# One product stage moved ahead of the mode sums, and an inverse transform split into five jobs, in a Fourier-layer kernel on one core

## The chip, the core and the metric

The kernel runs on 1 core of one Trainium2 chip. The metric is the device time of one launch in microseconds (us); less is better. TensorE does the matrix products (PE in the rows, PEld its weight loads), VectorE (DVE) and ScalarE (ACT) move and transform results, SyncE (SP) issues the transfers, and GpSimd (POOL) does almost nothing here. Everything is float32. One f32 product of the program is two matmul records and two weight-load records in the trace.

## What is computed

Thirty-two images of 8 x 256 x 256 go through two blocks, each added to its input. The first is a group norm and a masked 3x3 convolution with a hidden layer of 32. The second, which fills most of the time, is a group norm, a lift to 4 groups of 10 channels, four Fourier layers, and two pointwise products:

```
for i in range(4):
    h1 = _spectral_conv(h, sp_w1[i], sp_w2[i])
    h2 = _gconv1x1(h, w_w[i], w_b[i])
    h = h1 + h2
    if i < 3:
        h = _gswish(h, betas[i])
h = _gswish(_gconv1x1(h, fc1_w, fc1_b), betas[3])
return _gconv1x1(h, fc2_w, fc2_b)
```

`_spectral_conv` is a real 2D Fourier transform of which 24 x 12 modes are kept, a 10 x 10 complex product per group and mode, and the inverse transform. `_gconv1x1` is the mixing of the 10 channels of a group at each pixel.

## The kernel before

An image is worked through at a time, in a loop of 32 turns that all five engines run. Each engine has its own list of instructions, in an order written out by hand, and semaphores between them. For TensorE the order of one image is: the convolution (8 units), the first forward transform, then the four Fourier layers (`lay` 0 to 3), then fc1 and fc2 (128 steps).

A Fourier layer 1 to 3 begins with the spectrum that the layer before left. TensorE does `rows(lay, False)` and `rows(lay, True)` (L624), the second half of the forward transform, into bank 0. VectorE scales that (L1072 to L1074) and makes ten products of spectrum and weights (`next_modes`, L811), four buffers in a ring. TensorE adds them up as they come, in `mode_sums` (L555 and L558, 288 products of 24 per call of `summed`, 12 calls), into bank 1. Then VectorE copies the sums out and adds the bias (`mixed`, L1026, L1028), and for even layers turns them by a quarter (L1031 to L1038). While it does, TensorE runs `spin`, products whose result nobody reads (L566, bank 2).

The next stage is the one that the change is about, the inverse rows. `inverse_rows(lay)` makes 40 products (L588 in even layers, L584 in odd ones) in three jobs: job 0 into banks 0 to 3, job 1 into banks 4 to 7, job 2 (half as long) into banks 0 and 1. Each job is emptied into the tile `gst` by both engines at once, half of its banks each: ScalarE at L771, VectorE at L1046 (`inverse_kept`, whose slices come from `inverse_part`). Job 2 waits until job 0 has been emptied.

Then come 11 pixel units, `pixels(lay)`. A unit is a mixing part (L666, 16 products, the pointwise product of the layer on `hmem`, or on `lifted` in layer 0) and a Fourier part (L674, 8 products out of `gst`) that adds into the same four banks, 4 to 7 for even units and 0 to 3 for odd ones. ScalarE turns the four banks into the next `hmem` (L792). The mixing part of unit 0 waits for the emptying of job 1, whose banks it takes, and its Fourier part for the emptying of job 2. After unit 10 come `columns` (L605) and `rows`, which start the next layer.

`inverse_banks(t, engine)` says which banks an engine empties in job t, and `pixel_bank(lay, u)` which bank a unit begins with. The semaphore `s_g` counts jobs done, `s_gA` and `s_gD` jobs emptied by ScalarE and VectorE.

The functions in question, with the lines of the profile:

Of the kernel before, what the change touches and what calls it, by code (L numbers as in the profile page):

```python
# [14 lines left out]
LAYERS = 4  # L15
# [4 lines left out]
ROW2 = 2 * W  # L20
# [134 lines left out]
def program(nc, nb, x, conv1_w, conv1_b, conv2_w, conv2_b, lift_t, lift_b, lift_g, mix_w, mix_b, spec_w, betas,  # L155
            fc1_w, fc1_b, fc2_w, fc2_b, fwd_row, turn_id, fwd_col, inv_row, inv_col, grid, gridf, gmean, signs, out):
    with ExitStack() as ctx:
# [101 lines left out]
        WSP = 16 * 16  # L259

# [35 lines left out]
        def inverse_banks(t, engine):  # L296

            first, count = 4 * (t % 2), 4 if t < 2 else 2
            return (first, first + count // 2) if engine == 0 else (first + count // 2, first + count)

        def inverse_part(t, engine):

            b0, b1 = inverse_banks(t, engine)
            o = 4 * t + b0 % 4
            return (bass.AP(gst, NBLK * YY * o, [[128 * YY, 128], [NBLK * YY, b1 - b0], [32 * YY, 4], [1, NBLK * YY]]),
                    bass.AP(PS, 512 * b0, [[4096, 128], [512, b1 - b0], [NBLK * YY, 4], [1, NBLK * YY]]))
# [159 lines left out]
        def _(pe):  # L466
# [19 lines left out]
            with pe.Fori(0, nb) as i:  # L486
# [82 lines left out]
                def inverse_rows(lay):  # L569

                    n = (i * 4 + lay) * 3
                    pe.wait_ge(s_ot, i * 4 + lay + 1)
                    pe.sem_inc(s_bank, 1)
                    for t in range(3):
                        bank, count = 4 * (t % 2), 4 if t < 2 else 2
                        if t == 2:
                            pe.wait_ge(s_gA, n + 1)
                            pe.wait_ge(s_gD, n + 1)
                            pe.sem_inc(s_bank, 1)
                        for g in range(G):  # L580
                            for a in range(count):
                                p, ch = 64 * (a % 2), 5 * g + 2 * t + a // 2
                                if lay % 2:
                                    mm = nc.tensor.matmul(PS[32 * g:32 * g + MODES, bank + a, 0:4 * NBLK * YY],  # L584
                                                          rot[p:p + 32 + KX, ch, 0, 0:MODES], invr[p:p + 32 + KX, :], start=True,
                                                          stop=True, tile_position=(p, 32 * g))
                                else:
                                    mm = nc.tensor.matmul(PS[:, bank + a, NBLK * YY * g:NBLK * YY * g + NBLK * YY],  # L588
                                                          rot[p:p + 32 + KX, ch, :, :].rearrange("p c m -> p (c m)"),
                                                          invr[p:p + 32 + KX, 0:NBLK * YY], start=True, stop=True,  # L590
                                                          tile_position=(p, 0), skip_group_check=True)
                        mm.then_inc(s_g, 1)
# [48 lines left out]

                def pixels(lay):

                    for u in range(PU):
                        at = pixel_bank(lay, u)
                        if u >= 2:
                            before = u if at != pixel_bank(lay, u - 2) else u - 1
                            pe.wait_ge(s_hrow, i * (4 * PU) + (lay * PU + before))
                            if lay == LAYERS - 1:
                                pe.wait_ge(s_hlast, i * PU + before)  # L650
# [3 lines left out]
                        if lay == 0 and u in (0, 4):  # L654
                            pe.wait_ge(s_lnorm, i * 2 + 1 + u // 4)
                        pe.sem_inc(s_bank, 1)
                        for r in range(4):
                            for s in range(4):
                                if lay == 0:
                                    w, src = compw[32 * r:32 * r + 28, s, :], lifted[32 * r:32 * r + 28, u * ROW2:u * ROW2 + ROW2]  # L660
                                else:
                                    src = hmem[32 * r:32 * r + 30, s * PART + u * ROW2:s * PART + u * ROW2 + ROW2]
                                    w = mix13[32 * r:32 * r + 30, lay // 2, :]
                                if lay == 2:
                                    w = mix2[32 * r:32 * r + 30, s, :]
                                nc.tensor.matmul(PS[32 * s:32 * s + 32, at + r, :], w, src, start=True, stop=True,  # L666
                                                 tile_position=(32 * r, 32 * s))
                        if u == 0:
                            pe.wait_ge(s_gA, (i * 4 + lay) * 3 + 3)
                            pe.wait_ge(s_gD, (i * 4 + lay) * 3 + 3)  # L670
# [19 lines left out]
                for lay in range(LAYERS):  # L690
                    if lay:
                        mode_sums(lay)
# [47 lines left out]
        def _(act_):  # L740
# [26 lines left out]
            def inverse_kept(i, lay):  # L767
                for t in range(3):
                    act_.wait_ge(s_g, (i * 4 + lay) * 3 + (t + 1))
# [36 lines left out]
        def _(dve):  # L806
# [235 lines left out]
            def inverse_kept(i, lay):  # L1042
                for t in range(3):
                    dve.wait_ge(s_g, (i * 4 + lay) * 3 + (t + 1))
# [161 lines left out]
```

## Time and profile before

| | us |
|---|---|
| three runs | 17366.53, 17488.7, 17523.27 |
| their median | 17488.7 |
| the profiled execution | 17363.02 |
| its span, first to last instruction | 17361.2 |
| TensorE busy in it | 16419.9 (95%) |
| ScalarE busy | 11026.2 (64%) |
| VectorE busy | 6269.9 (36%) |
| mean granted TensorE clock | 0.971 |

The profiled execution is near the fastest of the three runs; the runs lie 157 us apart. Busy matmul time is modelled and says only that the engine had work in flight. A unit of work that comes once in each layer of each image comes 128 times, so 1 us there is 128 us, and 1 us in one layer of each image is 32 us.

### The profile page before, as it was taken

What the parts mean: (1) busy time and instruction counts of PE and PEld (TensorE: products, weight loads), DVE (VectorE), ACT (ScalarE), POOL (GpSimd) and SP (SyncE); (2) the same over time, 40 slices, a digit from 0 to 9 for tenths busy, and PEclk for the clock granted to TensorE, in tenths of its full rate; (3) what the DMA queues carried; (4) which work ended last, traced back from release to release, by engine and by line L of the source; (5) the groups of instructions that cost most, each with busy time, mean ns of one, the idle gap of its engine ahead of it and who ended that gap; (6) DMA issues with size and microseconds to landing.
All of it is one profiled execution on the core that took longest, in us unless ns stands there. A gap on an engine that the chain in (4) does not pass through costs nothing.

```text
span 17361.2 us, 558419 instructions
## 1 busy us (share of the span) xinstructions
PE 16419.9 (95%) x246998; PEld 6564.6 (38%) x246998; DVE 6269.9 (36%) x7495; ACT 11026.2 (64%) x10372; POOL 55.3 (0%) x69
## 2 busy tenths in 40 slices
PE   4999999999999999999999999999999999999999
PEld 2334433344433444333443334443344433344333
DVE  4234442234422344323443224442234432344322
ACT  1765567765576655676556676557665567655667
POOL 0000000000000000000000000000000000000000
PEclk9999999999999999999999999999999999999999
DMA  1111111111111111111111111111111111111111
GB/s 44 42 33 44 38 37 45 35 41 38 41 39 42 36 40 38 40 42 33 43 38 38 42 35 43 38 41 39 42 36 41 37 40 43 33 42 38 38 42 34
DMA packets 512312, 681.11 MB, mean 39 GB/s; under 512 B 90930, under 2 KB 483338, under 8 KB 493718
## 3 DMA queue, kind: packets, MB, share of 16 engines
q1 hardware_dynamic: 507318, 642.88, 14.4%
q8 instruction: 2046, 33.52, 0.8%
q14 instruction: 540, 4.42, 0.1%
q10 hardware_dynamic: 2408, 0.28, 0.0%
HBM read 507.57 MB, written 135.27 MB: 37 GB/s over the span
## 4 chain that ended last, share of the span: by engine, by line
PE 92%; DVE 4%; issue 2%; DVEq 1%; ACTq 1%; ACT 0%; SPq 0%; DMA 0%
PE PS L702 26%; PE PS L717 24%; PE PS L674 10%; PE PS L666 9%; PE PS L605 7%; PE PS L494 5%; PE PS L555 2%; PE PS L558 2%; PE PS L588 2%; PE PS L504 1%; PE PS L566 1%; PE PS L584 1%; PE PS L527 1%; PE PS L480 1%; PE PS L624 1%
## 5 line engine op out<-in xcount | busy, mean ns | idle before, releaser
L799 ACT ACTIVATE work<-PS 128x512 f32<-128x512 f32 (+1 forms) x8192 | 7939.5, 1021 | 762.9 <-PE PS L702 255.6
L702 PE MATMUL PS<-hmem,fcw 31*128 31x512 f32 x32768 | 4713.9, 645 | 106.9 <-DVE hmem L1109 45.4
L717 PE MATMUL PS<-work,fcw 128*32 128x512 f32 x32768 | 4398.8, 609 | 35.1 <-ACT work L799 33.4
L702 PEld LDWEIGHTS PS<-hmem,fcw 31*128 31x128 f32 x32768 | 1289.0, 184 | 3508.4 <-ACT work L799 3356.5
L792 ACT ACTIVATE hmem<-PS 128x2048 f32<-128x2048 f32 x1056 | 1983.1, 1878 | 663.6 <-PE PS L674 663.6
L1052 DVE STREAM_TRANSPOSE work<-hmem 128x2048 f32<-128x2048 f32 x864 | 1997.3, 2312 | 452.9 <-ACT hmem L792 405.8
L771 ACT ACTIVATE gst<-PS 128x528 f32<-128x528 f32 (+1 forms) x384 | 201.5, 539 | 2782.8 <-PE PS L584 1678.5
L674 PEld LDWEIGHTS PS<-invc,gst 24*128 24x128 f32 x22528 | 1495.7, 330 | 1189.1 <-issue 1188.5
L674 PE MATMUL PS<-invc,gst 24*128 24x256 f32 x22528 | 1917.8, 454 | 0.0
L717 PEld LDWEIGHTS PS<-work,fcw 128*32 128x32 f32 x32768 | 650.9, 108 | 3203.8 <-ACT work L799 3038.3
L1115 DVE SCALAR_TENSOR_TENSOR work<-PS,f2b,work 128x512 f32<-128x512 f32 x224 | 168.2, 751 | 4625.3 <-PE PS L717 4625.3
L666 PE MATMUL PS<-hmem,mix 30*32 30x512 f32 x33792 | 1228.7, 604 | 21.9 <-DVE gst L1046 21.9
L605 PE MATMUL PS<-work,fcol 32*24 32x512 f32 x30720 | 1183.4, 551 | 11.5 <-issue 10.3
L1115 DVE SCALAR_TENSOR_TENSOR wspec<-PS,f2b,wspec 128x512 f32<-128x512 f32 x128 | 96.1, 751 | 2935.7 <-PE PS L717 2935.7
L494 PE MATMUL PS<-work,c1w 32*64 32x512 f32 (+1 forms) x12288 | 824.7, 650 | 109.1 <-issue 95.3
L555 PE MATMUL PS<-work,sums 128*32 128x120 f32 x10240 | 720.7, 297 | 176.2 <-DVE work L811 164.6
L779 ACT ACTIVATE hmem<-PS,c1b 128x1024 f32<-128x1024 f32 x256 | 285.0, 1113 | 925.2 <-PE PS L494 925.2
L558 PE MATMUL PS<-work,sums 128*32 128x60 f32 x20480 | 723.5, 233 | 57.1 <-issue 56.7
L605 PEld LDWEIGHTS PS<-work,fcol 32*24 32x24 f32 x30720 | 641.8, 96 | 355.1 <-issue 134.1
L558 PEld LDWEIGHTS PS<-work,sums 128*32 128x32 f32 x20480 | 677.2, 118 | 88.0 <-issue 87.0
L555 PEld LDWEIGHTS PS<-work,sums 128*32 128x32 f32 x10240 | 617.7, 117 | 224.6 <-DVE work L811 189.8
L794 ACT ACTIVATE hmem<-PS 128x1024 f32<-128x1024 f32 x352 | 360.3, 1024 | 508.9 <-PE PS L674 508.9
(130 smaller groups left out, 9430.4 us busy)
## 6 DMA issues: line engine op xcount, KB each, us to landing
work<-in_x SPq DMA_DIRECT2D x1518, 128.0 KB, 2.5
wspec<-in_spec_w SPq DMA_DIRECT2D x768, 90.0 KB, 2.1
hmem<-x_d SPq DMA_DIRECT2D x128, 528.0 KB
x_d<-work SPq DMA_DIRECT2D x512, 128.0 KB, 2.9
wspec<-in_spec_w SPq DMA_DIRECT2D x768, 60.0 KB, 2.0
fcw<-fcw_d SPq DMA_DIRECT2D x32, 960.0 KB, 5.2
work<-x_d SPq DMA_DIRECT2D x384, 64.0 KB
wspec<-x_d SPq DMA_DIRECT2D x384, 64.0 KB
```

The lines of the kernel that those rows point to most:

```text
L494: mm = nc.tensor.matmul(to[:, :, lo:hi], c1w[32 * r:32 * r + 32, dx, :], rows[32 * r:32 * r + 32, 2 * u:2 * u + 2, lo + dx - 1:hi + dx - 1 ...
L555: nc.tensor.matmul(to[64 * t:64 * t + 32], sums[:, 0, pick, :], by[:, :, t:WID:2, :, s], start=begin, stop=end, tile_position=(0, 64 * t), ...
L558: mm = nc.tensor.matmul(to[64 * t + 32:64 * t + 64, 1 - r], sums[:, r, pick, :], by[:, r, t:WID:2, :, s], start=begin and r == 0, stop=end ...
L605: mm = nc.tensor.matmul(to, fcol[32 * r:32 * r + 32, b, :], part[32 * r:32 * r + 32, :, :, b, :], start=b == 0, stop=b == 7, tile_position ...
L666: nc.tensor.matmul(PS[32 * s:32 * s + 32, at + r, :], w, src, start=True, stop=True, tile_position=(32 * r, 32 * s))
L674: mm = nc.tensor.matmul(PS[:, at + r, y * W:y * W + W], gst[32 * r:32 * r + MODES, :, :, 2 * u + y].rearrange("p s o -> p (s o)"), invc[32 ...
L702: mm = nc.tensor.matmul(PS[:, fc_bank(p, r), :], f1w[32 * r:32 * r + 31, k, g, :], hmem[32 * r:32 * r + 31, g * PART + u * ROW2:g * PART + ...
L717: mm = nc.tensor.matmul(PS[32 * c:32 * c + 32, 7, :], f2w[:, k, g, :], act[p % 2][:, c * ROW2:c * ROW2 + ROW2], start=kg == 0, stop=final, ...
L792: nc.scalar.activation(unit(u), PS[:, at:at + 4, :], ACT.Silu).then_inc(s_hrow, 1)
L794: nc.scalar.activation(unit(u)[:, 0:2], PS[:, at:at + 2, :], ACT.Identity).then_inc(s_hrow, 1)
L799: nc.scalar.activation(act[p % 2][:, strips], PS[:, bank:bank + (3 if rest else 1), :].rearrange("p a b -> p (a b)"), ACT.Silu).then_inc(s ...
L1052: V.transpose(to, unit(u)).then_inc(s_tr, 1)
```

## The change

The inverse rows are done in five jobs of two banks instead of three jobs of four, four and two. Job t takes banks 0 and 1 if t is even and 2 and 3 if it is odd, and ScalarE empties the first of the two, VectorE the second. Jobs 2, 3 and 4 each wait until the job two before has been emptied. Banks 4 to 7 are free of the inverse rows. The mixing part of a unit is now a function of its own, `mix(lay, u)`. For layers 1 to 3 that of unit 0 is called ahead of `mode_sums(lay)`, into banks 4 to 7, where it lies until its Fourier part adds to it; in layer 0 it stays where it was, behind the inverse rows. The Fourier part of unit 0 waits until job 4 has been emptied, in all layers. The products are the same ones, in number and shape.

```diff
-            first, count = 4 * (t % 2), 4 if t < 2 else 2
-            return (first, first + count // 2) if engine == 0 else (first + count // 2, first + count)
...
+            return (bass.AP(gst, NBLK * YY * (2 * t + engine), [[128 * YY, 128], [32 * YY, 4], [1, NBLK * YY]]),
+                    bass.AP(PS, 512 * (2 * (t % 2) + engine), [[4096, 128], [NBLK * YY, 4], [1, NBLK * YY]]))
...
-                    pe.sem_inc(s_bank, 1)
-                    for t in range(3):
-                        bank, count = 4 * (t % 2), 4 if t < 2 else 2
-                        if t == 2:
-                            pe.wait_ge(s_gA, n + 1)
-                            pe.wait_ge(s_gD, n + 1)
-                            pe.sem_inc(s_bank, 1)
+                    for t in range(JOBS):
+                        if t >= 2:
+                            pe.wait_ge(s_gA, n + (t - 1))
+                            pe.wait_ge(s_gD, n + (t - 1))
+                        pe.sem_inc(s_bank, 1)
                         for g in range(G):
-                            for a in range(count):
-                                p, ch = 64 * (a % 2), 5 * g + 2 * t + a // 2
+                            for a in range(2):
+                                p, ch, bank = 64 * a, 5 * g + t, 2 * (t % 2) + a
...
                 def pixels(lay):

                     for u in range(PU):
                         at = pixel_bank(lay, u)
...
+                        if u or lay == 0:
+                            mix(lay, u)
                         if u == 0:
-                            pe.wait_ge(s_gA, (i * 4 + lay) * 3 + 2)
-                            pe.wait_ge(s_gD, (i * 4 + lay) * 3 + 2)
...
+                            pe.wait_ge(s_gA, (i * 4 + lay) * JOBS + JOBS)
+                            pe.wait_ge(s_gD, (i * 4 + lay) * JOBS + JOBS)
                             pe.sem_inc(s_bank, 1)
...
                     if lay:
+                        mix(lay, 0)
                         mode_sums(lay)
                     spin(2, 3 if lay % 2 == 0 else 1)
                     inverse_rows(lay)
```

## Rows read from the trace of the kernel before

**Rows 1.** The page's head, and its first lines of busy time and chain.

```profile
span 17361.2 us, 558419 instructions
...
PE 92%; DVE 4%; issue 2%; DVEq 1%; ACTq 1%; ACT 0%; SPq 0%; DMA 0%
```

**Rows 2.** What TensorE waited for: us in total, times, longest.

```profile
PE PS L555 <- DVE work L811: 164.6, 96, 1.7
...
PE PS L558 <- issue: 56.7, 67, 1.5
...
PE PS L666 <- DVE gst L1046: 21.9, 64, 0.4
```

**Rows 3.** Chain at the end of `mode_sums`, layer 1: start, us, what.

```profile
8378.28 1.13 issue
8379.41 0.26 PE PS L558
```

**Rows 4.** Windows of `mode_sums`, layers 1, 2, 3: length, PE busy, PEclk; sums of 32.

```profile
sum 292.91, PE 218.98; mean PE 6.84
...
402.02:409.42 7.40, 6.43 (x289) 1.00 0.01 2
936.27:945.28 9.01, 7.50 (x289) 0.81 0.01 2
...
sum 259.39, PE 230.54; mean PE 7.20
...
sum 254.13, PE 221.07; mean PE 6.91
```

**Rows 5.** Window up to the first pause of layer 1, L555, then L558.

```profile
8371.70:8375.25 3.55, 3.49 (x54) 1.00 0.02 5
...
8371.70:8375.25 3.55, 3.46 (x107) 3.17 (x107) 1.00 0.02 5
```

**Rows 6.** Transfer queues of the page: packets, MB, share.

```profile
q8 instruction: 2046, 33.52, 0.8%
```

**Rows 7.** Timeline of the inverse rows of layer 1 (odd): start, us, engine.

```profile
8380.83 2.83 PE L584 MATMUL PS<-invr,work 56*24 56x264 f32 x80
8382.14 0.71 DVE L1046 COPY gst<-PS 128x528 f32<-128x528 f32 x1 [1.49 <-PE PS L584]
...
8383.19 1.05 DVE L1046 COPY gst<-PS 128x528 f32<-128x528 f32 x2 [0.34 <-PE PS L584]
...
8384.00 1.15 PE L666 MATMUL PS<-hmem,mix 30*32 30x512 f32 x32 [0.34 <-DVE gst L1046]
8385.08 0.63 PE L674 MATMUL PS<-invc,gst 24*128 24x256 f32 x4
```

**Rows 8.** Timeline of the inverse rows of layers 0 and 2 (even).

```profile
8323.20 4.68 PE L588 MATMUL PS<-invr,work 56*128 56x66 f32 x80 [0.74 <-DVEq L1039]
...
8329.17 1.36 PE L674 MATMUL PS<-invc,gst 24*128 24x256 f32 x16
...
8443.68 0.43 DVE L1046 COPY gst<-PS 128x264 f32<-128x264 f32 x1 [0.18 <-PE PS L588]
```

**Rows 9.** Chain, inverse rows of layer 2, of image 15 and then of 14.

```profile
8438.96 4.68 PE PS L588 x80
8443.65 1.11 PE PS L666 x32
8444.75 1.29 PE PS L674 x16
...
7897.68 6.46 PE PS L588 x80
7904.14 1.94 PE PS L666 x32
7906.08 2.06 PE PS L674 x16
```

**Rows 10.** Window of the units in layer 2, image 14; PEclk behind the counts.

```profile
7902.20:7914.20 12.00, 12.00 (x151) 0.51 0.23 57
```

More of the change, by code:

```diff
@@ L587, in inverse_rows @@
                                 else:
-                                    mm = nc.tensor.matmul(PS[:, bank + a, NBLK * YY * g:NBLK * YY * g + NBLK * YY],
+                                    mm = nc.tensor.matmul(PS[:, bank, NBLK * YY * g:NBLK * YY * g + NBLK * YY],
                                                           rot[p:p + 32 + KX, ch, :, :].rearrange("p c m -> p (c m)"),
@@ L640, in mode_sums, with mix @@
                         mm.then_inc(s_sum, 1)
+                def mix(lay, u):
+                    at = pixel_bank(lay, u)
+                    if u >= 2:
+                        before = u if at != pixel_bank(lay, u - 2) else u - 1
+                        pe.wait_ge(s_hrow, i * (4 * PU) + (lay * PU + before))
+                        if lay == LAYERS - 1:
+                            pe.wait_ge(s_hlast, i * PU + before)
+                    if lay == 0 and u in (0, 4):
+                        pe.wait_ge(s_lnorm, i * 2 + 1 + u // 4)
+                    pe.sem_inc(s_bank, 1)
+                    for r in range(4):
+                        for s in range(4):
+                            if lay == 0:
+                                w, src = compw[32 * r:32 * r + 28, s, :], lifted[32 * r:32 * r + 28, u * ROW2:u * ROW2 + ROW2]
+                            else:
+                                src = hmem[32 * r:32 * r + 30, s * PART + u * ROW2:s * PART + u * ROW2 + ROW2]
+                                w = mix13[32 * r:32 * r + 30, lay // 2, :]
+                            if lay == 2:
+                                w = mix2[32 * r:32 * r + 30, s, :]
+                            nc.tensor.matmul(PS[32 * s:32 * s + 32, at + r, :], w, src, start=True, stop=True,
+                                             tile_position=(32 * r, 32 * s))
                 def pixels(lay):
@@ L767, in inverse_kept @@
             def inverse_kept(i, lay):
-                for t in range(3):
-                    act_.wait_ge(s_g, (i * 4 + lay) * 3 + (t + 1))
+                for t in range(JOBS):
+                    act_.wait_ge(s_g, (i * 4 + lay) * JOBS + (t + 1))
                     dst, src = inverse_part(t, 0)
@@ L1042, in inverse_kept @@
             def inverse_kept(i, lay):
-                for t in range(3):
-                    dve.wait_ge(s_g, (i * 4 + lay) * 3 + (t + 1))
+                for t in range(JOBS):
+                    dve.wait_ge(s_g, (i * 4 + lay) * JOBS + (t + 1))
                     dst, src = inverse_part(t, 1)
```

32 lines of the change are left out of this document (3 added, 29 removed).

## The prediction

> **What bounds the kernel.** I read the page's head and chain first, then what TensorE waited for, then the order of events in one image. The chain that ends last lies on TensorE for 92% of the span [rows 1], so only time in which TensorE stands or works alone can be won. Between the layers it does stand. Before each of the 96 `mode_sums` (3 layers of 32 images) it waits for the first product of VectorE, 164.6 us in all, 1.71 us each [rows 2]. Inside `mode_sums` it pauses for 56.7 us in all with nothing named as releaser [rows 2]. Before the mixing part of unit 0 in the odd layers it waits for an emptying, 21.9 us in 64 times [rows 2]. The reader should see two places: the gap of 1.71 us, which holds no TensorE work, and the stretch from the inverse rows to the first Fourier part, where the mixing part lies on the path.
>
> Everything below is per image and times 32. The sum is made against the profiled execution, 17363.02 us, span 17361.2 [rows 1], which is 126 us below the median of 17488.7. The median is the better guess for a new set of runs, so the gain is taken off the median.
>
> **Mixing part into the gap.** It lasts 1.15 us [rows 7] and the gap 1.71 [rows 2], so 0.56 us are left over and it costs nothing there. Its operands are `hmem`, finished before the columns, and weights. Its banks 4 to 7 were last read when `rows(lay, True)` was allowed to start. It waits for nothing, and VectorE, which makes the product meanwhile, reads bank 0. If it did not fit, the excess would be paid in full; the bounds are 0 and 0.2 us for its last records ahead of the sums. I take 0. SyncE gets no new wait.
>
> **Inverse rows in odd layers, before.** From the first product (8380.83) to the first Fourier part (8385.08) are 4.25 us [rows 7]. The mixing part is in it for 1.08 and hides the emptying of job 2.
>
> **The same, after.** A job is 16 of the 80 records. The first matmul to the emptying's start is 1.31 us for 32 records [rows 7]; 80 records start within 2.83 minus 0.38 us (one record's own length in that group), some 0.03 each, so a job of 16 starts emptying 0.75 to 0.85 us after its first record. The emptying is 0.43 us for 264 columns [rows 8], and from its end to the next record of TensorE pass 0.10 us (8383.19 + 0.71 to 8384.00) [rows 7]. Jobs 0, 2 and 4 therefore follow at 1.28 to 1.38 us, with jobs 1 and 3 between them in the shadow. The first Fourier part starts after 3 such turns, 3.84 to 4.14 us. That is 0.11 to 0.41 less than 4.25, I take 0.35, the lower end of the turn, since the short job 2 of before is the same burst; times 64 layers, 22 us. Note how little that is of 1.15: the last emptying, until now hidden behind the mixing part, comes onto the path.
>
> **Layer 2.** Before, 8438.96 to 8444.75, 5.79 us in the chain [rows 9]. After, the 80 records take 4.68 [rows 9], then 0.04 to the emptying, 0.43 [rows 8] and 0.10, together 5.25. A job here lasts 0.9 us, longer than 0.43 + 0.14 behind its end, so jobs 2 to 4 wait for nothing. Gain 0.5, times 32, 16 us. In both kinds of layer more waits stand in TensorE's queue; behind each stands only the next job.
>
> **Layer 0.** The mixing part stays but no longer needs job 1 emptied. Before, 8323.20 to 8329.17, 5.97 us [rows 8]; layer 2 shows 5.79 or a little less for the same work. After, 4.68 and 1.11 less the overlap: 5.7. Gain 0.25, times 32, 8 us. Job 4's emptying is hidden by the mixing part. This first term is 46 us.
>
> **`mode_sums`: the instruction list.** This term I find larger. Nothing in these sums is changed, but they don't run at their own speed. Their mean lengths are 292.91 / 32 = 9.15 us in layer 1, 8.11 in layer 2, 7.94 in layer 3 [rows 4], for identical work. In layer 1 TensorE pauses 1.13 us right before the last of the 288 products' records, and VectorE waits for that one [rows 3]. An earlier pause comes after record pair 54 + 107 = 161 [rows 5]. Counting weight loads in all images, the pauses of layer 1 are always behind 161 and 287 of 288, in layer 2 behind 254, in layer 3 behind 218. 161 and 287 are 126 apart. The instruction queue moved 33.52 MB in 2046 packets, 16 KB each [rows 6]; 493996 matmul and load records in 2046 packets are 241 each, or 120 pairs and some semaphore work. So a pause is the arrival of a piece of TensorE's instruction list, some 126 pairs, at a fixed place of the program. Within the sums these pieces come 3.5 us apart at the least, while TensorE would use one up in 2.4 to 3.
>
> Moving 16 products (32 pairs) to the front shifts every place in the sums of that layer by 32, and the added waits by another 2 (layer 1) to 6 (layer 3). The places become about 0, 126 and 252 in layer 1, 92 and 218 in layer 2, 54 and 180 in layer 3. So layer 1 gets the places that layer 2 has now, and layer 2 those of layer 3; the pause before the very last record goes. By that alone layer 1 falls from 9.15 to layer 2's 8.11 and layer 2 from 8.11 to 7.94: 1.21 us, 39 us in all.
>
> The Trainium skill, page "Runtime: NRT & Kernel Launch", section "Instruction fetch mechanics", says that instructions come in 16 KiB blocks of 256 and that crossing a boundary is "mostly hidden". The block size agrees with the 16 KB of the queue; the hiding doesn't, since the 56.7 us stand in the waits. By the page's rule this part of the term would be nothing and the gain 39 us less.
>
> **`mode_sums`: the clock.** Full speed is PEclk 1.00 (2.4 GHz), 0.50 is 1.2 GHz. In 55 of the 96 windows of sums the mean is below 1 (14, 23 and 18 by layer), such as 0.81 beside 1.00 in the two of layer 2 shown [rows 4]. The fall comes 1.4 to 3 us into the sums and lasts 3.41 us; what stood before was the gap of 1.71 us. In layer 2 the windows with a full clock average 7.45 us and the others 8.36, in layer 3 7.56 and 8.24. With the mixing part in it, the gap is 0.56 us. I expect the fall to go. Then layer 1 is at about 7.5 (layer 2's clean value), layer 2 at 7.56 and layer 3 at 7.45: 1.65 + 0.55 + 0.49 = 2.69 us, 86 us with the instruction part in it. The bounds are 39 (no effect on the clock) and 86.
>
> **Sum.** 46 + 86 = 132 us; 17488.7 - 132 = 17357. On the profile's own scale that is 17231. It is 0.76% of the median.
>
> **Rivals.**
>
> A, the clock still falls. The half clock then costs the sums what it does now. For it: a gap of 0.6 us remains, and sums of narrow products are thin work. Gain 46 + 39 = 85, 17404.
>
> B, only the rearrangement counts. The blocks' arrival then paces the whole stretch from the rows to the first Fourier part, so 32 pairs more ahead of the sums are paid in them, and the clock falls as before. For it: the pieces arrive 3.5 us apart in layer 1 already. Against it: in the gap of 1.71 us nothing is used up. Gain 46, 17443.
>
> C, slower. The clock falls in the inverse rows of the even layer 2, and stays low through the units. In image 14 (counted from 0) this happens: inverse rows 6.46 us for 4.68, unit 4.00 (1.94 + 2.06) for 2.40 [rows 9], PEclk 0.51 over 12 us [rows 10]. Over the 13.65 us that it lasts, that costs 1.8 + 1.6 x 2.4, some 5.6 us. It is so in 4 of 32 images, 8, 14, 25 and 30. After the change the dense mixing part behind the inverse rows is gone and TensorE stands for 0.57 us there, which speaks for it. Against it: the odd layers never did it, and 28 images of layer 2 did not. In all 28 others it costs 157 us; against a gain of 132 that is 25 us slower, 17514. It decides from 24 more falls (132 / 5.6); if layers 1 and 3 fell so as well, it would be over 1% slower.
>
> D, more than forecast. The runs of before lie 157 us apart, as much as 28 falls of the kind in C. If a gap like the one that is filled is what brings the slower runs about, they go too, and the gain is 132 plus up to half the spread: 17280.
>
> E, the change doesn't do what it says: the waits of jobs 2 to 4 add 0.5 us to each odd turn pair, so that the first term is 64 x 1 us worse. Then 86 + 46 - 64 = 68, 17421. The rows give each emptying room, so the chance is small.
>
> **Chances.** Forecast 0.48, A 0.19, B 0.09, C 0.07, D 0.12, E 0.05. About 1% (175 us) is what a measurement of this kernel can tell from no change. The forecast lies 43 us inside it; with runs that spread by 157 us it can show as more, which I give a third of D's and a quarter of the forecast's weight on top of D. Faster by over 1%: 0.26; within 1%: 0.70; slower by over 1%: 0.04. The range goes from 17205 (the profile's own time less 132 and half of D's extra) to 17450, just over B. C is left out.
>
> **What would show it.** In the new profile: the wait of L555 for L811 falls from 164.6 to about 54 us; the wait of L558 for issue from 56.7 to under 25; the pause before the last record of layer 1 is gone; the windows of `mode_sums` average 7.5 in all three layers, with PEclk 1.00; L666 no longer waits for L1046, but L674 does, 0.5 us in each of 96 layers; first inverse product to first Fourier part 3.9 us in odd layers and 5.25 in layer 2. The prediction is wrong if the pauses turn up at another place of the sums, above all right before their last record in layer 3, where my count puts the next boundary 16 pairs behind the end; or if half-clock stretches follow the inverse rows.

## The result

| | before | after |
|---|---|---|
| median of 12 runs, us | 17380.17 | 17558.23 |
| lowest to highest | 17342.17 to 17562.06 | 17422.08 to 17598.48 |
| profiled execution, its span | 17363.02, 17361.2 | 17491.19, 17489.3 |
| granted clock in it | 0.971 | 0.965 |

The ratio is 1.008, 95% interval 1.0048 to 1.0113: slower by 0.8%, where 0.76% faster was forecast. The median of before was 17380 in these 12 runs and not 17489 as in the three runs that the forecast started from, so ratios are the measure below. Executions over 1.5% above the fastest of their kernel are left out of the ratios, among them three at 30044.58, 31264.92 and 53764.4 us. A record is one matmul of the trace; the 288 of `mode_sums` are records, of 144 products. Line numbers of after: L549 and L552 are the mode sums, L576 and L580 the inverse rows, L669 the Fourier part, L654 the mixing part, L1042 the emptying on VectorE.

The page of after, head and chain, beside [rows 1]:

```profile
span 17489.3 us, 559923 instructions
...
PE 91%; DVE 4%; issue 2%; DVEq 1%; ACTq 1%; ACT 0%; SPq 0%; DMA 0%
```

What TensorE waited for in after, beside [rows 2]: us in total, times, longest.

```profile
PE PS L549 <- DVE work L807: 61.4, 96, 0.7
PE PS L669 <- DVE gst L1042: 58.6, 96, 0.6
...
PE PS L549 <- issue: 53.1, 64, 1.5
...
PE PS L669 <- issue: 21.0, 32, 0.9
...
PE PS L552 <- issue: 14.7, 21, 1.1
```

The gap shrank as forecast, from 164.6 to 61.4 us, and the last emptying stands on the path as forecast, 0.6 us in each of 96 layers. But the pauses of the mode sums did not shrink: 53.1 + 14.7 = 67.8 us, while before had 56.7 on L558 and 10.1 on L555, together 66.8. And there is a new one of 21.0 us, in 32 Fourier parts.

Windows of `mode_sums` of after, layers 1, 2, 3 (columns as in [rows 4]). A window runs from the start of VectorE's first product, 0.7 us ahead of TensorE's first record, to VectorE's copy of the sums:

```profile
350.33:357.81 7.48, 6.39 (x299) 1.00 0.02 4
...
sum 250.60, PE 204.62; mean PE 6.39
...
sum 242.72, PE 207.34; mean PE 6.48
...
sum 248.17, PE 199.98; mean PE 6.25
```

Together 741.5 us, where [rows 4] have 806.4. So this stage did gain 65 us, and all 96 windows have the full clock. Now the stage behind it. The units of a layer, from the first Fourier part to the end of unit 10, take 25.10 us at full clock. The same windows of after, layers 2 and 3:

```profile
422.52:457.32 34.80, 34.80 (x507) 0.66 0.05 12
968.83:993.94 25.11, 25.11 (x508) 1.00 0.11 26
...
sum 908.41, PE 908.38; mean PE 28.39
...
486.18:512.68 26.50, 25.93 (x496) 1.00 0.35 62
1023.31:1051.59 28.28, 27.42 (x496) 0.94 0.25 58
...
sum 905.92, PE 884.80; mean PE 27.65
```

Layer 2 is at full speed in one image and at PEclk 0.66 in another. Layer 3 is 1.4 us too long even where the clock is full, and longer still where it isn't. Over the four layers the units take 813.8, 839.8, 908.4 and 905.9 us; before they took 803.2, 803.3, 813.5 and 803.1. That is 245 us lost. With 65 us gained in the sums and 34 in the inverse stage it leaves 146 us more; the spans differ by 128.

Why layer 3 is too long even at full clock is in the chain of image 15 (start, us, what):

```profile
8568.86 0.74 PE PS L576 x16
8569.60 0.02 issue
8569.62 0.44 DVE gst L1042
8570.07 0.09 issue
8570.16 0.74 PE PS L576 x16
...
8572.23 0.45 DVE gst L1042
8572.67 0.09 issue
8572.76 1.36 PE PS L669 x16
8574.12 1.08 PE PS L654 x32
8575.20 1.27 PE PS L669 x11
8576.47 0.59 issue
8577.06 0.86 PE PS L669 x5
```

The turns of 1.30 us and the 3.90 from 8568.86 to 8572.76 are those of the forecast. But behind 16 + 32 + 11 records of the units TensorE pauses, at this same record in all 32 images. The next piece of its instruction list (one packet of queue q8) is on its way only then. The transfer view of 8574.2 to 8575.2, image 15 (there is no such line for 8568.86 to 8574.2):

```profile
q8 instruction: 1, 0.02, 5.8%
```

In that stretch SyncE has just issued 960 KB of `fcw` and 24 reads of 64 KB.

### The profile page after: what moved, and what is told of

It reads as the page before. It is cut to its first block, busy times and chain, and to the rows that moved or that the text cites. A ratio compares the mean times of both kernels' runs of the same rounds, so it can differ in the third digit from the quotient of the medians.

```text
span 17489.3 us, 559923 instructions
## 1 busy us (share of the span) xinstructions
PE 16568.8 (95%) x246998; PEld 6485.1 (37%) x246998; DVE 6304.5 (36%) x7751; ACT 11074.1 (63%) x10628; POOL 55.3 (0%) x69
## 4 chain that ended last, share of the span: by engine, by line
PE 91%; DVE 4%; issue 2%; DVEq 1%; ACTq 1%; ACT 0%; SPq 0%; DMA 0%
PE PS L698 25%; PE PS L713 23%; PE PS L669 11%; PE PS L654 9%; PE PS L597 7%; PE PS L488 5%; PE PS L549 2%; PE PS L580 2%; PE PS L498 1%; PE PS L552 1%; PE PS L576 1%; PE PS L616 1%; PE PS L521 1%; PE PS L474 1%; PE PS L560 1%
## 5 line engine op out<-in xcount | busy, mean ns | idle before, releaser
L669 PE MATMUL PS<-invc,gst 24*128 24x256 f32 x22528 | 2045.6, 472 | 79.6 <-DVE gst L1042 58.6
L669 PEld LDWEIGHTS PS<-invc,gst 24*128 24x128 f32 x22528 | 1560.6, 330 | 1336.9 <-issue 1325.0
L767 ACT ACTIVATE gst<-PS 128x264 f32<-128x264 f32 x640 | 250.7, 392 | 2710.1 <-PE PS L576 1619.9
L654 PE MATMUL PS<-hmem,mix 30*32 30x512 f32 x33792 | 1316.2, 649 | 0.0
L549 PE MATMUL PS<-work,sums 128*32 128x120 f32 x10240 | 660.5, 275 | 122.9 <-DVE work L807 61.4
L552 PE MATMUL PS<-work,sums 128*32 128x60 f32 x20480 | 655.5, 219 | 15.1 <-issue 14.7
L1059 DVE STREAM_TRANSPOSE work<-PS 128x640 f32<-128x640 f32 (+1 forms) x768 | 455.9, 649 | 525.2 <-PE PS L597 525.2
L549 PEld LDWEIGHTS PS<-work,sums 128*32 128x32 f32 x10240 | 540.5, 108 | 230.3 <-DVE work L807 148.6
```

The costliest lines, as they stand in the source:

```text
L549: nc.tensor.matmul(to[64 * t:64 * t + 32], sums[:, 0, pick, :], by[:, :, t:WID:2, :, s], start=begin, stop=end, tile_position=(0, 64 * t), ...
L552: mm = nc.tensor.matmul(to[64 * t + 32:64 * t + 64, 1 - r], sums[:, r, pick, :], by[:, r, t:WID:2, :, s], start=begin and r == 0, stop=end ...
L669: mm = nc.tensor.matmul(PS[:, at + r, y * W:y * W + W], gst[32 * r:32 * r + MODES, :, :, 2 * u + y].rearrange("p s o -> p (s o)"), invc[32 ...
L1059: V.transpose(part[0:high, size * g:size * g + size], src)
```

## The experiments

A fall below is an image in which the granted clock was under 1 in some part of inverse rows and units of the layer. Sums and units are means over the 32 images of the one profiled execution, worked out from such windows; in the two shifted kernels the windows of the sums hold 1.2 us of added increments. Ratios compare runs made beside each other on one chip. They come from several such sets, in which the median of before itself went from 17357.88 to 17550.29 us, so two ratios of different sets that lie 1% apart need not tell two kernels apart.

| kernel | ratio (95%) | sums, layers 1, 2, 3 | units, 1, 2, 3 | falls, layers 0 to 3 |
|---|---|---|---|---|
| before | | 9.15 8.11 7.94 | 25.10 25.42 25.10 | 0 5 4 0 |
| after | 1.008 (1.0048, 1.0113) | 7.83 7.59 7.76 | 26.24 28.39 28.31 | 3 10 19 15 |
| five_jobs_only | 1.0107 (1.0022, 1.0192) | 9.34 7.77 7.51 | 31.23 26.50 25.21 | 0 30 13 0 |
| five_jobs_late_all | 1.008 (1.0042, 1.0118) | 9.31 7.86 7.66 | 31.95 26.10 25.12 | 0 30 14 0 |
| five_jobs_wide | 0.9874 (0.9837, 0.9911) | 9.45 8.01 7.67 | 25.50 25.70 25.12 | 0 2 6 0 |
| five_jobs_shifted | 1.0193 (1.0179, 1.0208) | 10.13 9.51 9.05 | 27.25 25.75 27.69 | 3 18 11 11 |
| after_filled | 0.9983 (0.9949, 1.0017) | 7.80 7.55 8.00 | 25.11 25.25 25.70 | 0 0 8 0 |
| after_late_loads | 0.9968 (0.9934, 1.0002) | 7.91 7.60 7.61 | 26.05 28.01 25.66 | 1 6 21 0 |
| after_late_all | 0.9963 (0.9923, 1.0003) | 7.86 7.55 7.78 | 26.05 29.48 25.77 | 1 8 26 0 |
| after_filled1_late_all | 0.9925 (0.9888, 0.9961) | 7.93 7.67 7.73 | 25.10 26.39 25.12 | 0 0 14 0 |
| after_late_spin4 | 0.9906 (0.9872, 0.9941) | 7.95 7.76 7.72 | 25.43 27.98 26.00 | 0 3 25 0 |
| after_filled1_late_spin4 | 0.9896 (0.9829, 0.9964) | 7.95 7.69 7.91 | 25.10 25.10 25.69 | 0 0 0 0 |
| before_gap_filled | 0.9915 (0.9884, 0.9946) | 8.60 7.84 7.15 | 25.10 25.12 25.12 | 0 0 1 0 |
| before_gap_spin4 | 0.989 (0.9863, 0.9917) | 8.78 7.45 7.33 | 25.10 25.10 25.13 | 2 2 0 0 |
| before_mix_twice | 0.9999 (0.9951, 1.0046) | 7.77 7.67 7.83 | 25.10 26.07 25.10 | 1 0 11 0 |
| before_wait_job1 | one run | 9.15 8.16 7.88 | 25.11 27.42 25.13 | 4 0 24 0 |
| before_shifted | 1.0071 (1.0057, 1.0085) | 10.00 9.25 9.00 | 25.10 25.20 25.60 | 1 0 2 0 |
| five_wide_gap_spin4 | 1.0 (0.9963, 1.0038) | 8.71 7.38 7.47 | 25.10 25.10 26.73 | 0 1 0 2 |

**five_jobs_only.** One half of the change alone.

```diff
                     if lay:
-                        mix(lay, 0)
                         mode_sums(lay)
...
-                        if u or lay == 0:
-                            mix(lay, u)
+                        mix(lay, u)
```

> The kernel after, but the mixing part of unit 0 stands behind the inverse rows in all four layers; the inverse rows stay in five jobs. Theory 1 (the clock falls because the dense mixing part no longer stands right behind the thin inverse rows, and TensorE stands for 0.6 us there instead): the falls behind the inverse rows go back to 4 to 10 of 128 layers from 47, the half-clock stretches in the gap of 1.71 us before the mode sums come back (some 55 of 96), and the time is that of before, ratio to before 0.995 to 1.003. Rival (the five jobs with their waits thin out the inverse rows themselves): the falls stay at 30 or more and the ratio is 1.004 or more. In layer 1 the pause before the last record of the mode sums comes back, since the 32 pairs are no longer ahead of it.

The chain behind the inverse rows of layer 1, image 15:

```profile
8506.25 0.67 PE PS L576 x16
8506.92 1.11 PE PS L654 x32
8508.04 0.79 PE PS L668 x5
8508.83 0.97 issue
8509.79 1.80 PE PS L668 x11
```

Five jobs alone lose as much as the whole change: Theory 1 fell, and the rival's numbers came. There is a pause of 0.97 us, before the same record in all 32 images, and 30 falls in layer 1. The piece of the list for it set out 3.6 us or more behind the first inverse product; in before it set out at 1.25 to 1.78. But 27 of the 30 falls begin 6.7 us or later behind the first inverse product, so behind the pause and not inside the rows. Layer 3 has the same jobs and the same stops between them, no such pause, and no fall in 32 images.

**after_filled** puts products whose result nobody reads between job 4 and the Fourier part.

```diff
                         if u == 0:
+                            if lay:
+                                pe.wait_ge(s_gA, (i * 4 + lay) * JOBS + JOBS - 1)
+                                pe.wait_ge(s_gD, (i * 4 + lay) * JOBS + JOBS - 1)
+                                pe.sem_inc(s_bank, 1)
+                                spin(2, 2)
```

> The kernel after, with two spin products (128 x 504, into bank 2, result not read) between job 4 of the inverse rows and the Fourier part of unit 0 in layers 1 to 3, as soon as job 3 has been emptied. Theory 1: the place where TensorE stood is dense again, the falls behind the inverse rows drop from 47 to under 15, and the time falls by 100 to 190 us against the kernel after, ratio to before 0.992 to 1.000, the spins themselves costing 0.3 us in each of 96 layers (29 us). Rival (the falls come from the late instruction block of layer 3 and from the inverse rows themselves): the falls in layers 1 and 2 stay, the ratio is 1.006 to 1.011. The 1.29 us pause in layer 3 stays by both.

44 falls of layers 1 to 3 became 8, although the filler costs 1.2 to 1.45 us a layer where 0.3 were expected. The pause in layer 3, expected to stay, is nearly gone as well: the boundary now stands before record 45, where two records are at most 0.55 us apart; in after they were 1.06 apart on average. So for layer 3 this run does not part the filler from the pause.

**after_late_loads** lets SyncE issue `fcw` and the residual rows when 6 units of layer 3 are done.

```diff
-                sp_.wait_ge(s_ot, i * 4 + 4)
+                sp_.wait_ge(s_hrow, i * (4 * PU) + (3 * PU + 6))
                 sp_.dma_start(fcw[:, 0:FCW], fcw_d[:, :]).then_inc(s_fcw, 16)
```

> The kernel after, but SyncE issues the load of fcw (960 KB) and the residual loads behind it only when 6 units of layer 3 are done, in place of right after the last mixing of modes. Theory 2 (the piece of the instruction list that TensorE asks for at the start of layer 3's inverse rows is held up by these loads until 5.5 us, where 1.6 would be usual): the packet comes at 1.5 to 2 us, the pause of 1.29 us before weight load 59 of the units in layer 3 is gone in all 32 images, and the half-clock falls in layer 3 (15, most of them starting 8.8 to 10.6 us behind the first inverse product) drop to under 5; 40 us for the pause and 40 to 60 for the clock, ratio to before 1.001 to 1.004. Rival (the block is late for another reason): the pause stays at its place and the ratio at 1.008. If fc1 must wait for the load, its first wait grows; 5.2 us of loading against some 11 us of units left speak against that.

Layer 3's units, two windows and the sum:

```profile
477.65:503.31 25.66, 25.66 (x496) 1.00 0.27 68
1011.96:1037.37 25.41, 25.41 (x496) 1.00 0.28 67
...
sum 821.15, PE 820.76; mean PE 25.65
```

905.9 us became 821.2. In this kernel the piece sets out 4.9 us behind the first inverse product (median) and not 5.35 to 6.26; 1.5 to 2 were expected. TensorE no longer pauses, and the 15 falls of layer 3 are gone.

**before_gap_filled** is the kernel before with `spin(2, 2)` ahead of the mode sums of layers 1 to 3.

> The kernel before, with two spin products (into bank 2, result not read) in the gap ahead of the mode sums of layers 1 to 3; nothing else is changed. It splits my two terms of the mode sums. Clock term: the half-clock stretches in the mode sums (55 of 96) go; layer 2 falls from 8.1 to 7.5 us and layer 3 from 7.9 to 7.6. Instruction term: the program's places move by only 4 pairs, so the pauses of layer 1 stay (at 157 and 283) and it stays at 8.9. Together 1.2 us an image, 38 us, ratio to before 0.997 to 0.999. Rival (filling the gap ahead of the sums moves the half-clock stretches to the inverse rows or units behind them, as the sum of the clock's rest is paid somewhere): half-clock falls in the inverse rows and units rise from 9 of 128 layers to over 25 and the ratio is 1.003 or more.

No fall in any of the sums (55 before), and the falls of layers 1 and 2 nearly gone too: half of what the change was after, at a price of nothing. The profiled execution is 88 us shorter than that of before, where 38 were expected; the ratio of 0.9915 owes the rest to before, whose 25 runs beside it went up to 17567.97 us.

**five_jobs_late_all** is five_jobs_only with the transfers late in all layers; **after_late_all** and **after_filled1_late_all** do the same to after, the last with `spin(2, 1)` as filler.

```diff
-                    sp_.wait_ge(s_ot, i * 4 + l)
+                    sp_.wait_ge(s_hrow, i * (4 * PU) + ((l - 1) * PU + 6))
```

> Five jobs with the mixing part of unit 0 kept behind the inverse rows in all layers, as in five_jobs_only; besides, the transfers that SyncE issued when the spectrum was turned (weights of the next spectral product, in layer 3 the convolution's weights and the residual rows) go out when 6 of the 11 units before them are done. Theory H (a piece of TensorE's instruction list is held up by these transfers, TensorE pauses for it behind the inverse rows, and the clock falls in the units of that layer): the pause of 1.68 us in layer 1 goes (32 x 1.68 = 54 us), the falls of layer 1 go from 30 to under 10, its units from 31.23 to about 25.8 us; 17605 - 54 - 120 = 17430, ratio to before about 1.003. Rival T (the clock falls because five jobs with waits are thin work, whatever the list does): the pause may go, the units of layer 1 stay at 29 us or more, ratio 1.007 or more.

Theory H fell for layer 1: with no transfer in the way the piece still set out at 3.6 us, the pause and the 30 falls stayed. The late transfers take the pause away in layer 3 of after alone.

> The changed kernel with all transfers of that moment issued later, in layers 1 and 2 too. Theory H: in layers 1 and 2 of the changed kernel no piece of the list is held up, only layer 3 has the pause of 1.29 us; so this gives what after_late_loads gave, ratio 0.997, units 26.0, 28.0 and 25.6 us in layers 1 to 3. Rival M (the transfers slow the stretch itself, by memory traffic on the tiles that it reads): layers 1 and 2 lose their falls as well, units 25.2 each, 120 us less, ratio 0.990.

As H said for layers 1 and 3; layer 2 came to 29.48 us for 28.0. M is out.

> The changed kernel with all transfers later and half the filler of after_filled (2 spin records' worth of products in place of 4) between job 4 and the first Fourier part of layers 1 to 3. Theory G (the falls of layers 1 and 3 come from the empty 0.5 us and the waits behind the thin inverse rows; any dense work there keeps the clock): falls 0 in layers 1 and 3, units 25.2, the filler costs 0.6 us a layer, so 17432 (after_filled) - 0.6 x 96 - 41 (its pause in layer 3) = 17333, ratio 0.993. Rival F (half the filler is too little): falls of layers 1 and 2 as in after_late_loads, 10 and more, ratio 0.999 or more.

G holds where it can be seen: one product, at 0.35 us, took layer 1 from 8 falls to 0 (layer 3 had none left). The 14 falls of layer 2 begin 2.2 to 3.1 us behind the first inverse product, where no filler has yet come.

**before_mix_twice** adds to the kernel before a copy of unit 0's mixing part ahead of the mode sums; its result is overwritten.

```diff
                     if lay:
+                        mix_ahead(lay)
                         mode_sums(lay)
```

> The kernel before with a copy of the mixing part of unit 0 in the gap ahead of the mode sums of layers 1 to 3, its result thrown away; the inverse stage stays three jobs and has its own mixing part. This is the mode-sums half of the change alone. My forecast for it was 86 us less. Theory S (the half that the mode sums gain is independent of what is lost behind the inverse rows): sums 7.8, 7.6 and 7.7 us as in the changed kernel, units 25.1 to 25.3 in all layers, inverse stage as before; the gain is that of before_gap_filled with 13 us more, ratio 0.990 to 0.992. Rival L (the shift of the instruction list by 32 pairs is what loses time behind the inverse rows): units of 26 us or more in layers 1 to 3, ratio 1.000 or more.

The sums gain what S said, within 0.15 us, and the ratio is 1.0 all the same, where S said 0.990 to 0.992. Layer 2 has 11 falls, and the inverse stage of layer 1 takes 5.02 us for 4.49. Its timeline, image 15:

```profile
8400.25 2.83 PE L584 MATMUL PS<-invr,work 56*24 56x264 f32 x80
8403.42 2.04 PE L676 MATMUL PS<-hmem,mix 30*32 30x512 f32 x32 [0.34 <-DVE gst L1057]
```

The mixing part takes 2.04 us; in [rows 7] it takes 1.15. The piece boundaries that moved out of one stage have moved into the next.

**five_jobs_wide** keeps the five jobs of five_jobs_only and gives them four pairs of banks.

```diff
-                        if t >= 2:
-                            pe.wait_ge(s_gA, n + (t - 1))
-                            pe.wait_ge(s_gD, n + (t - 1))
+                        if t == 4:
+                            pe.wait_ge(s_gA, n + 1)
+                            pe.wait_ge(s_gD, n + 1)
...
-                                p, ch, bank = 64 * a, 5 * g + t, 2 * (t % 2) + a
+                                p, ch, bank = 64 * a, 5 * g + t, 2 * (t % 4) + a
...
                 def mix(lay, u):
+                    if u == 0:
+                        pe.wait_ge(s_gA, (i * 4 + lay) * JOBS + 4)
+                        pe.wait_ge(s_gD, (i * 4 + lay) * JOBS + 4)
```

> five_jobs_only with four pairs of banks in place of two, so that only job 4 waits (for job 0); unit 0's mixing part waits for job 3. In five_jobs_only TensorE's next piece of instructions set out 3.6 to 4.4 us after the first inverse product, in the kernel before at 1.3. Theory W (the piece is asked for when TensorE's own list has been read up to a certain place, and the waits of jobs 2 and 3 stop the reading short of it): it sets out at 1.3 to 1.7 us again in layer 1, the pause of 1.68 us in layer 1 is gone, the falls of layer 1 go from 30 to under 10 and its units from 31.2 to under 26.5; ratio about 1.000. Rival P (the piece comes late because of where the list stands, not because of the waits): pause of 1.6 us and units of 31 us stay, ratio 1.008. Rival T (thin work alone makes the clock fall): the pause goes, but units of layer 1 stay over 29 us.

The chain of layer 1, image 15, beside that of five_jobs_only:

```profile
8356.33 2.08 PE PS L576 x64
8358.41 0.02 issue
8358.43 0.45 DVE gst L1043
8358.88 0.09 issue
8358.97 1.15 PE PS L657 x32
8360.12 1.44 PE PS L671 x16
```

No turn between jobs, no pause, 3.79 us to the first Fourier part, and the dense mixing part is where it was. 30 falls became 2. Both of the 2 begin 0.2 us behind the first inverse product, like the 5 of before, so none is of the kind that followed the pause. Same five jobs, same products: TensorE stops for banks once, where the chain of five_jobs_only has two stops between jobs, and the piece sets out at 1.4 to 2.2 us again, as W said. The ratio is lower than the 1.000 that W gave. The Trainium skill, page "TensorE: Matmul & The Clock Gate", section "A second HAM failure mode: psum-queue depth-cycling", tells of another kernel in which PSUM banks are cycled through, TensorE is idle for moments between the groups of matmuls, and the clock goes up and down. The counts of layer 1 look like it, 30 falls on two pairs of banks and 2 on four, but the pause went with the stops; layer 3 of five_jobs_only cycles over two pairs too and has 0 falls, so the cycling by itself is not shown to lower the clock here.

**after_late_spin4**, **after_filled1_late_spin4** and **before_gap_spin4** lengthen the filler ahead of the even layers' inverse rows.

```diff
-                    spin(2, 3 if lay % 2 == 0 else 1)
+                    spin(2, 4 if lay % 2 == 0 else 1)
```

> The changed kernel with all transfers later (after_late_all) and 4 instead of 3 products in the filler ahead of the even layers' inverse rows. That filler leaves 0.74 us empty before the first inverse product. Theory Q (the 26 falls of layer 2, most of which begin 2.2 to 3.1 or 5.0 to 6.7 us after the first inverse product, need that empty 0.74 us ahead of the thin work): falls of layer 2 under 8, units 25.9 us for 29.5, at a cost of 0.2 us in each even layer; 17404 - 32 x 3.6 + 13 = 17300, ratio 0.990. Rival N (they come from what lies in and behind the inverse rows): falls of layer 2 stay near 20, ratio 0.997.

Mixed. Layer 2 still had 25 falls, but all begin 5.0 us or later, behind the rows; those inside the rows are gone.

> after_filled1_late_all with 4 instead of 3 products in the filler ahead of the even layers' inverse rows. Its 14 falls of layer 2 all begin inside the inverse rows, 2.2 to 3.1 us behind the first product. Theory Q: they go, units of layer 2 25.1 for 26.4, inverse stage 6.1 for 6.8; 17347 - 32 x 2.0 + 13 = 17296, ratio 0.990. Rival N: the falls stay at 10 or more, ratio 0.993 or more.

Q holds: no fall in any layer. So, with the transfers late, two empty places make the falls of layer 2, the 0.74 us ahead of the inverse rows and the 0.6 us behind them, and each filler cures its own.

> before_gap_filled with 4 instead of 3 products in the filler ahead of the even layers' inverse rows. It had 1 fall in layer 2. Theory Q and rival N alike: no gain there; the filler costs 0 to 0.2 us in each even layer, 0 to 13 us; ratio 0.991 to 0.993 as it was. Only if the falls of 5 us ahead of layer 0's inverse rows (28 of 32 images) also end sooner would it be 0.988 or less.

No gain over before_gap_filled that these runs could tell.

**before_wait_job1** adds one wait to the kernel before, and nothing else.

```diff
                         for g in range(G):
+                            if t == 1 and g == 2:
+                                pe.wait_ge(s_gA, n + 1)
+                                pe.wait_ge(s_gD, n + 1)
+                                pe.sem_inc(s_bank, 1)
                             for a in range(count):
```

> The kernel before with one wait more and nothing else: in the middle of job 1 of the inverse rows (behind load record 48 of 80) TensorE waits until job 0 has been emptied, which job 1 itself does not need. Theory W (waits stop the reading of TensorE's list and so hold up the request for its next piece): in layer 1 the piece that set out 1.3 us behind the first inverse product sets out at 2.5 us or later. The stop itself is 0.4 to 0.6 us an odd layer, some 30 us in all. Rival P (place alone): it sets out at 1.3 to 1.7 us as before.

Theory W, in the form that any wait holds the piece up, fell: it set out at 1.23 to 1.84 us. But look at layer 2, where the wait held TensorE for 0.18 us only. The sum of its units' windows, and in the page's head the span:

```profile
sum 877.44, PE 877.44; mean PE 27.42
```

24 falls in place of 4, and 17542.3 us of span. Whether the stop does it is not shown: this is one execution, at a granted clock of 0.966, and of the 13 of before beside it four took 17495 to 17535 us at 0.964 to 0.966, with no trace that would show their falls.

**five_jobs_shifted** and **before_shifted** add 24 semaphore increments to TensorE's list ahead of the mode sums and change no work.

```diff
                     if lay:
+                        for _ in range(24):
+                            pe.sem_inc(s_bank, 1)
                         mode_sums(lay)
```

> five_jobs_only with 24 semaphore increments more in TensorE's list ahead of the mode sums of layers 1 to 3, in the gap; they do nothing, but every place where a piece of the list begins comes 12 record pairs earlier in layer 1, 24 in layer 2 and 36 in layer 3. Theory P (which record the piece boundary and its request fall on decides the pause and with it the falls): the pause of 1.68 us in front of record 38 of the units of layer 1 moves or goes, and the falls of layer 1 go from 30 to under 15, units from 31.2 to under 28; ratio to before 1.003 or less. Rival T (five jobs with their waits are what loses the clock, wherever the list stands): 25 falls or more in layer 1, ratio 1.009.

> The kernel before with the same 24 increments. This prices the shift of the list by itself, which my forecast called a gain. Forecast's theory: boundaries of the mode sums go from 161 and 287 to about 149 and 275 in layer 1, 254 to 230 in layer 2, 218 to 182 in layer 3; sums 0.2 to 0.5 us shorter in layer 1, no falls more behind the inverse rows than the kernel before has (0, 5, 4, 0), ratio 0.997 to 1.000. Rival: the shift puts a boundary behind the inverse rows, falls of 15 or more in one of the layers, ratio 1.004 or more.

The boundaries went where the count put them: from 286 to 274 and 160 to 148 in layer 1 of the one, from 287 to 275 in the other. The pause behind layer 1's inverse rows went from record 38 to 27, but stayed (32 images, about 1.9 us between two records). The piece now set out at 2.72 to 3.15 us, about 1.0 behind the start of job 3 (1.75) where in five_jobs_only it was 1.0 behind that of job 4 (2.60). That fits a request that goes out at a place in the list, once a wait ahead of it has ended; it rests on these two kernels. Neither theory is clean: the falls of layer 1 went from 30 to 18, but layer 3 got a pause in all images and 11 falls. Both theories gave a smaller ratio than the 1.0193 measured. The increments themselves lengthened the gap by about 1.2 us a layer, 115 us in 96 layers, which is most of the 0.7% of before_shifted. Less that, its sums are up to 0.35 us shorter than those of before, and layers 1 to 3 have no more falls, as the forecast's theory had it. Their wait in five_jobs_shifted:

```profile
PE PS L549 <- DVE work L807: 285.9, 96, 3.1
```

That row names VectorE, but the increments stand between.

**five_wide_gap_spin4** joins the remedies: five jobs on four pairs, `spin(2, 2)` in the gap, `spin(2, 4)` in even layers.

> five_jobs_wide with two filler products in the gap ahead of the mode sums of layers 1 to 3 and 4 instead of 3 ahead of the even layers' inverse rows. Each part is measured by itself; if they add, the mode sums lose their 56 falls (before_gap_filled: 9.15, 8.10, 7.94 became 8.60, 7.84, 7.15 us) and layer 2 its 6: 533.4 us an image less 1.7 less 1.0, 530.7; ratio 0.982, 17235 us on the chip where five_jobs_wide took 17315. Rival: the clock's falls only move to the next thin place; ratio 0.987 as five_jobs_wide.

They did not add. Its ten runs go from 17309.44 to 17499.9 us, median 17424.43; five_jobs_wide had 17315.12 on the same chip. The profiled one is among the fastest and has hardly a fall, yet its units of layer 3 are too long at the full clock:

```profile
470.95:497.23 26.28, 26.11 (x506) 1.00 0.27 64
1007.31:1033.61 26.30, 26.11 (x505) 1.00 0.25 65
```

A boundary lies before record 77 of these units and TensorE pauses there in 27 images. Why other runs are up to 180 us longer, at clocks down to 0.969, no profile shows.

## Why the prediction was wrong

**Mixing part into the gap: right.** It cost nothing there; 61.4 / 96 = 0.64 us of the gap are left, 0.56 were forecast.

**Inverse rows in odd layers: right.** 3.91 us for a forecast of 3.9. The windows of layer 1, from the first product to the first Fourier part:

```profile
sum 125.01, PE 93.12; mean PE 2.91
```

**Layers 2 and 0: right where the clock held** (5.26 us for 5.25 in image 1 of layer 2), but the mean of layer 2 is 5.94, as the clock fell inside the rows, and layer 0 is 5.96 for 5.7 (5.68 in the 29 images without a fall). The term of 46 us came to 34.

**The instruction list: the places right, the worth wrong.** The boundaries came at 254, 219 and 180, as counted (252, 218, 180). But they cost the same 67 us in the sums as before, and what the forecast did not follow is that a list of equal pieces has its boundaries moved everywhere: the change put one of them behind 59 records of layer 3's units, where the piece came late. It was priced as a gain of its own, 39 us, with the wait for issue to fall under 25 us; that wait is 67.8. before_mix_twice shows what it is worth alone with the clock part: nothing.

**The clock in the sums: right.** 55 falls became 0. The sums came to 7.83, 7.59 and 7.76 us for about 7.5; 65 us of 86.

**The failed step is rival C's "Against it: the odd layers never did it, and 28 images of layer 2 did not".** On it the sum has no term for the units behind the rows, which came out 245 us longer. The forecast took the inverse rows of before, with a dense mixing part behind them and one wait inside, as evidence for rows without the one and with three of the other. (Layer 1 of before has 5 falls in the table; they begin within 0.4 us of the first inverse product and leave its units at 25.10, so the reading of the trace was right.) The mechanism of C was read from the trace and its break-even, 24 falls, worked out; after has 47. Of the 245 us some 45 are layer 3's 1.4 us at full clock; the other 200 are at most 4.3 a fall, for 5.6 in C. What the runs showed in its place: in layer 1 the empty time behind job 4 brings the falls (8 of after_late_all, 0 with one product of filler). In layer 3 the late piece of the list does (15 falls, 0 in after_late_loads, where the empty time is still there); whether the empty time has a part is not shown. In layer 2 it is the empty places on both sides of the rows. Each count is of one execution; the ratios, 1.008 for after, 0.9963 with the transfers late and 0.9896 with the places filled too, go the same way. With both filled and the transfers late, the change as made is at 0.9896. C should have had the largest chance beside the forecast, with all layers in it, and the range should have held it.

**E was the wrong way to look at the waits.** The waits cost no time of their own (14.5 us on L576 for the turns of two layers); that they cost by making the stage thin is not shown, since layer 3 of five_jobs_only has them and no fall. In its layer 1 they seem to hold up the piece of the list: with one stop, in five_jobs_wide, it came early again.

**D: open.** The spread of before follows the clock (17342 to 17562 us in these 12 runs), but a filled gap did not always narrow it: before_gap_filled spans 17275.29 to 17349.23, five_wide_gap_spin4 190 us. The slower executions of before were not traced.

**Slips in the numbers.** The lower end of the range is the profile's 17231 less half of D's extra, which gives 17192 and not 17205. The shares named for a gain of over 1% (all of D, a third of it and a quarter of the forecast's) add up to 0.28, not 0.26. The pieces of the list come 3.3 us apart in the sums at the least, not 3.5. None of this bears on the miss.

## What to carry to other kernels

Work that moves off the critical path is not only its own time: if it was the dense work between two thin stages, price what the clock does without it, by the falls that the trace already shows, in every layer that is made alike. When TensorE's list is shifted, follow each boundary through the whole loop, not through the stage in hand, and see what SyncE transfers when the next piece is asked for. Try the cheap form first: two filler products in the gap gave 0.9915 with none of the rearrangement. With one more ahead of the even layers' rows (before_gap_spin4, 17319.88 us) it is not told apart from five jobs on four pairs of banks (17315.12) or the change with all places filled (17303.9), measured beside it.

## What was not expected of the hardware

One unread product in 0.6 us of empty time behind the inverse rows took the falls of layer 1 from 8 to 0 of 32, and two in a gap of 1.71 us took those of the sums from 55 to 0 of 96. One q8 packet is a boundary: TensorE's list is cut into pieces of 126 record pairs, and 24 increments moved the boundaries of layer 1 by 12. The Trainium skill, page "Runtime: NRT & Kernel Launch", section "Instruction fetch mechanics", calls the crossing "mostly hidden"; in this kernel it is in most of the loop, but in the mode sums, and behind waits, TensorE stands for up to 1.6 us. A piece set out about 1.0 us behind the end of the wait that stood before its request (3.6 behind 2.60, 2.72 behind 1.75), and later still, 5.35 to 6.26 us, when 960 KB and 24 reads went out at the same moment. Which place of a piece asks for the next is not settled: in before_wait_job1 a wait behind record 48 did not hold it up, in five_jobs_only one of three did.
